# Keys and values of the second cross attention projected in the first one and kept in DRAM, and the first attention's tiles done two by two

## The reference

```python
def xattn0(x, ctx, mask):          # 4 heads of 64
    q = x @ Wq; k, v = split(ctx @ Wkv)
    s = where(mask, q k^T * 64**-0.5, -inf)
    return softmax(s) v @ Wo
def xattn1(x, ctx):                # 16 heads of 16, no mask
    q = x @ Wq1.T + bq; k = ctx @ Wk1.T + bk; v = ctx @ Wv1.T + bv
    return softmax(q k^T * 16**-0.5) v
x = x + xattn0(layernorm(x), ctx, mask)
x = x + gated_delta_net(layernorm(x))
x = x + top1_experts(layernorm(x))
x = x + xattn1(layernorm(x), ctx)
x = x + linear_attention(layernorm(x))
x = x + top2_experts(layernorm(x))
```

## Time and profile before

| | us |
|---|---|
| median of 3 runs | 1309.65 |
| lowest and highest | 1301.12, 1310.67 |
| profiled execution, its own time | 1307.67 |
| its span, first to last instruction | 1305.9 |
| first attention, first T to last value | 9 to 397 |
| delta net and first experts | 398 to 560 |
| second attention, preparation | 560 to 633.6 |
| its first load issued by SP, in the first experts | 543.9 |
| second attention, chunks 0 to 13 | 633.6 to 1251 |
| rest | 1251 to 1306 |

### The profile page before, as it was taken

The page is one execution under the profiler, slowest core; times in us unless marked ns, Lnnn a source line. Parts: engine busy times, 40 slices in busy tenths (PEclk is TensorE's granted clock), DMA queues, the critical chain, the costliest instruction groups (busy, mean ns, idle before and its releaser), DMA issues. The chain is left out here.

```text
span 1305.9 us, 25471 instructions
## 1 busy us (share of the span) xinstructions
PE 1134.1 (87%) x9184; PEld 714.7 (55%) x9184; DVE 574.0 (44%) x1415; ACT 601.2 (46%) x1233; POOL 224.9 (17%) x257
## 2 busy tenths in 40 slices
PE   7999999999998379775689889988988988988966
PEld 4666666666666179541355554554555545555543
DVE  3333333333336984345146436534534633634524
ACT  2544455444555412331355545544645544645631
POOL 1000000000004342203123213303312312321000
PEclk9999999999998789797789989988988988989976
DMA  4233111400000000229975585566557557537000
GB/s 156 81 127 115 32 33 34 127 32 32 0 0 1 1 1 2 65 63 166 218 123 101 108 137 96 112 111 113 101 101 125 96 93 130 100 65 120 2 1 5
DMA packets 64879, 101.98 MB, mean 78 GB/s; under 512 B 14366, under 2 KB 55350, under 8 KB 62102
## 3 DMA queue, kind: packets, MB, share of 16 engines
q1 hardware_dynamic: 64790, 100.67, 38.0%
HBM read 80.32 MB, written 19.60 MB: 77 GB/s over the span
## 5 line engine op out<-in xcount | busy, mean ns | idle before, releaser
L1539 DVE TENSOR_REDUCE mx<-bank 128x1 f32<-128x512 f32 (+1 forms) x448 | 257.2, 618 | 223.3 <-PE bank L1432 222.3
L1621 ACT ACTIVATE p<-bank 128x512 f32<-128x512 f32 x392 | 234.3, 598 | 180.6 <-PE bank L1470 174.7
L1470 PE MATMUL bank<-qrows,krows 99*128 99x128 bf16 x1568 | 161.2, 228 | 45.1 <-DMA qrows<-n3T 35.1
L1484 PE MATMUL bank<-p,v 128*32 128x128 f32 x3136 | 172.7, 293 | 19.6 <-issue 16.2
L1432 PE MATMUL bank<-krows,qrows 96*128 96x512 bf16 (+1 forms) x448 | 161.0, 363 | 13.7 <-DMA krows<-kscr 10.9
L1470 PEld LDWEIGHTS bank<-qrows,krows 99*128 99x128 bf16 x1568 | 116.3, 101 | 95.6 <-issue 52.4
L1303 POOL TENSOR_TENSOR kt<-kf,kt 128x512 bf16<-128x512 f32 (+1 forms) x52 | 53.7, 1034 | 449.6 <-ACT kt L1605 449.6
L1484 PEld LDWEIGHTS bank<-p,v 128*32 128x32 f32 x3136 | 63.4, 110 | 117.9 <-issue 88.6
L468 DVE CUSTOM_DVE_ANT_0 sc<-bank,pen 128x448 f32<-128x448 f32 x112 | 65.7, 620 | 113.9 <-issue 113.9
L1415 PE MATMUL bank<-ctxT,WT 128*128 128x512 f32 (+1 forms) x224 | 97.2, 557 | 3.7 <-ACT kt L1605 1.7
L1440 PE MATMUL bank<-WT,ctxT 128*128 128x256 f32 x392 | 98.2, 391 | 2.1 <-ACT v L1295 1.4
(11 more groups left out here) (292 smaller groups left out, 1449.7 us busy)
## 6 DMA issues: line engine op xcount, KB each, us to landing
ctx<-ctx SPq DMA_DIRECT2D x28, 896.0 KB, 10.8
krows<-kscr SPq DMA_DIRECT2D x84, 256.0 KB, 8.5
krows<-kscr SPq DMA_DIRECT2D x84, 192.0 KB, 6.9
kscr<-kt SPq DMA_DIRECT2D x14, 768.0 KB, 3.6
kscr<-kt SPq DMA_DIRECT2D x14, 576.0 KB, 13.0
ew<-L_ffn_expert_w SPq DMA_DIRECT2D x1, 2048.0 KB, 10.6
ew<-L_ffn_We SPq DMA_DIRECT2D x1, 2048.0 KB, 15.9
mask<-mask_BxSxS_bf SPq DMA_DIRECT2D x14, 112.0 KB, 5.2
```

The lines of the kernel that those rows point to most:

```text
L1470: ins = pe.matmul(bank[ST1[u % 2]][:, i * P:(i + 1) * P], krows[half][:, s, krow(h), cols], qrows[:, s, h, :], start=True, stop=True)
L1484: ins = pe.matmul(bank[OT1][32 * i:32 * i + 32, j * P:(j + 1) * P], v1[:, s, t, h * (D1 + 1):h * (D1 + 1) + 32], p1[:, u % 4, i * P:(i + 1 ...
L1539: dve.tensor_reduce(mx1[:, h, half:half + 1], bank[SM1[k % 3]][:, 0:HW[half]], AX.X, ALU.max).then_inc(S("smread1"), 1)
L1621: act.activation(p1[:, u % 4, :], bank[ST1[u % 2]][:], ACT.Exp).then_inc(S("exp1"), 1)
```

## The change

1. In the first attention, for each chunk, four operations J0 to J3 are added (keys of the second attention, 512 and 384 columns; ACT adds the bias and writes `kf`, POOL makes all three bf16 parts), and V becomes V0 to V6, one per tile and 512 columns wide (256 of the first attention's values, 256 of the second's), each copied out by two ACT copies. SP stores each chunk's key parts and values to DRAM, for all 14 chunks.
2. Per step, tiles go in pairs: the sides of two tiles, two `turn_exps`, two `values`. K, J and V share the two `KV` banks, 15 operations a chunk.
3. The second attention has no T, K, V, no context load and no store. `krows` and `v1` have three slots. `l1_loads`, in the first experts, gathers all of chunks 0, 1 and 2. S is one operation per head over both halves (two banks, one DVE reduction of 896 columns). Units go in pairs. The chunk loop is written out. M of the next chunk stands in pair 8 of 14; S8 to S15 of the next chunk in pairs 0 to 6, S0 to S7 of the one after it in pairs 7 to 13.
4. The weights of the second attention are loaded and turned at the start of the first.

```diff
+        PLAN0 = ((("T0", "T1"), ("T2", "T3")), (("K0", "K1"), ("K2", "K3")), (("S0", "S1"), ("J0", "S2", "S3")),
+                 (("S4", "S5", "V0"), ("J1", "S6", "S7", "M0")), (("V1", "E0", "E1", "E2", "E3"), ("V2", "V3")),
+                 (("J2",), ("V4", "V5")), (("V6", "F0"), ("J3",)))
+        TPAIRS = ((0, 1), (2, 3), (4, 5), (6,))
...
+                def kv_free(op, c):
+                    i = KVO.index(op)
+                    if some(NKV * c + i - 1):
+                        pe.wait_ge(S("kvread0"), NKV * c + i - 1)
...
+                    elif op[0] == "J":
...
+                        for i in range(DC):
+                            ins = pe.matmul(bank[kv_bank(op, s)][:, 0:HW[half]], WTk[:, i, b * P:(b + 1) * P],
+                                            ctxT0[:, i, HO[half]:HO[half] + HW[half]], start=(i == 0), stop=(i == DC - 1))
...
-                        for t in range(nt):
-                            for i in range(DC):
-                                ins = pe.matmul(bank[KV[k % 2]][:, t * D:(t + 1) * D],
-                                                ctxT0[:, i, (t0 + t) * P:(t0 + t + 1) * P], Wkv0[:, i, D:2 * D],
+                        for i in range(DC):
+                            ins = pe.matmul(bank[kv_bank(op, s)][:], ctxT0[:, i, k * P:(k + 1) * P],
+                                            Wv01[:, i].rearrange("p w o -> p (w o)"),
...
+                    for ts in TPAIRS:
+                        for t in ts:
+                            for op in PLAN0[t][0] + PLAN0[t][1] if ahead else ():
+                                side(op, c + 1, 1 - s, n + s)
+                        for t in ts:
+                            if t + 2 < CT:
+                                turn_exps(c, s, t + 2)
+                        for t in ts:
+                            values(c, s, t)
...
         def l1_loads(sp):
+            gather(sp, 0, 0)
+            gather(sp, 0, 1)
             for half in range(2):
                 sp.dma_start(krows[half][KROWS:KONES].rearrange("p s h (r c) -> p (s h r) c", c=P),
-                             onesb[KROWS:KONES].unsqueeze(1).to_broadcast([3, 2 * H1 * HT[half], P])
+                             onesb[KROWS:KONES].unsqueeze(1).to_broadcast([3, R1 * H1 * HT[half], P])
                              ).then_inc(S("krows_ones"), 16)
+            fetch_values(sp, 0)
+            for c in range(1, R1):
+                gather(sp, c, 0)
+                gather(sp, c, 1)
+                fetch_values(sp, c)
...
+                for c in range(NCH):
+                    if R1 <= c + 2 < NCH:
+                        sp.wait_ge(S("st1"), UNITS * c)
+                        gather(sp, c + 2, 1)
+                        sp.wait_ge(S("pv1"), UNITS * c)
+                        fetch_values(sp, c + 2)
+                    if c + 1 < NCH:
+                        rows(c + 1)
                     if c + 3 < NCH:
+                        sp.wait_ge(S("st1"), UNITS * c + HT[0] * 4)
+                        gather(sp, c + 3, 0)
...
+                def score(c, h):
+                    r, b = c % R1, sm_bank(("S", c, h))
+                    if h == 0:
+                        for half in range(2):
+                            pe.wait_ge(S(f"krows{half}_{r}"), 16 * NJ * (c // R1 + 1))
```

More of the change, by code:

```diff
@@ L507, in _ @@
                 penalty(0, 0, 0)
[L508 removed]
+                for op in PRO0:
                     side(op, 0, 0, 0)
@@ L560, in take_exps @@
                     act.wait_ge(S("pt0"), CT * c + t + 1)
-                    if some(CT * c + t - 1):
-                        act.wait_ge(S("pv0"), CT * c + t - 1)
-                    u = (s + t) % 2
-                    act.copy(pT0[:, u, :], bank[PT[u]][:]).then_inc(S("pT0"), 1)
-                for op in ALL0:
+                    was = CT * c + t - (2 if t < 3 else 3)
+                    if some(was):
+                        act.wait_ge(S("pv0"), was)
+                    act.copy(pT0[:, t % 4, :], bank[PT[(s + t) % 2]][:]).then_inc(S("pT0"), 1)
+                for op in PRO0:
                     side(op, 0, 0, 0)
@@ new lines, in sm_free @@
+                def sm_free(op):
+                    i = SMPOS[op] - 2
+                    if i >= 0:
+                        kind, c, h = SMSEQ[i]
+                        if kind == "S":
+                            pe.wait_ge(S("smread1"), H1 * c + h + 1)
+                        elif kind == "M":
+                            pe.wait_ge(S("n3T1"), c + 1)
+                        else:
+                            pe.wait_ge(S("acc1"), 2 * c + 3)
+                def score(c, h):
+                    r, b = c % R1, sm_bank(("S", c, h))
+                    if h == 0:
+                        for half in range(2):
+                            pe.wait_ge(S(f"krows{half}_{r}"), 16 * NJ * (c // R1 + 1))
+                    sm_free(("S", c, h))
+                    for half in range(2):
+                        ins = pe.matmul(bank[b + half][:, 0:HW[half]], qrows[0:KROWS, 0, h, :],
+                                        krows[half][0:KROWS, r, krow(h), :], start=True, stop=True)
+                    ins.then_inc(S("sm1"), 1)
@@ L1425, in side, with scores @@
+                def side(kind, c, h):
+                    if kind == "S":
+                        score(c, h)
+                    elif kind == "M":
+                        turn_maximum(c)
+                    else:
+                        turn(c)
+                def scores(c, u):
+                    t, j, g = u // 4, u % 4, UNITS * c + u
+                    if u == 0:
+                        if c == 0:
                             pe.wait_ge(S("krows_ones"), 32)
-                        if isinstance(c, int) and c == 1 and k == 0:
+                        if c == 1:
@@ L1510, in _ @@
-                steps1(pe, step)
+                ln_pe(pe, "ln2", 4)
+                pe.wait_ge(S("ln2_hT"), 1)
+                for b in range(DC):
+                    for i in range(DC):
+                        ins = pe.matmul(bank[5][:, b * P:(b + 1) * P], WTq[:, i, b * P:(b + 1) * P],
+                                        hT[:, i, :], start=(i == 0), stop=(i == DC - 1))
+                ins.then_inc(S("q1_psum"), 1)
+                pe.wait_ge(S("qrows_in"), 16 * NJ)
+                for op in PRO1:
+                    side(*op)
@@ new lines, in _ @@
+                scores(0, 0)
+                scores(0, 1)
+                for c in range(NCH):
+                    for p in range(PAIRS):
+                        if p + 1 < PAIRS:
+                            scores(c, 2 * p + 2)
+                            scores(c, 2 * p + 3)
+                        elif c + 1 < NCH:
+                            scores(c + 1, 0)
+                            scores(c + 1, 1)
+                        for op in plan1(c, p):
+                            side(*op)
+                        values(c, 2 * p)
+                        values(c, 2 * p + 1)
@@ L1579, in step @@
+                ln_dve(dve, "ln2")
+                query()
+                for op in PRO1:
+                    side(*op)
+                for c in range(NCH):
+                    if some(c):
                         read_out(c - 1)
-                        rescale(c - 1, 1 - s)
-                    sides(side, ALL1, c, s, n, two, one)
-                steps1(dve, step)
+                    for p in range(PAIRS):
+                        for op in plan1(c, p):
+                            side(*op)
```

663 lines of the change are left out of this document (284 added, 379 removed), and 6 rows, old and new, of the table PLAN1.

## The result

The changed kernel takes 1315.98 us, the kernel before 1307.08 (medians of seven runs each on the same chip); the ratio is 1.0076, with a 95% interval of 1.0048 to 1.0104. The forecast was 1293 us, most likely faster. The measured time lies inside its range of 1248 to 1325; direction and likeliest case were wrong. The profiled execution took 1318.36 us, its span is 1316.6.

What follows compares the result with a forecast made beforehand. The prediction took both attentions to be PE-bound before the change, and the second paced by its gather cycle after. 1307.67 + 182 + 29 - 226 = 1292.7, so 1293 us, range 1248 to 1325.

Steps and rivals of the forecast that it cites:

- First attention, +182: First attention: added J and wider V paid in full on PE, 13 us more a chunk; +182 us, bounds +150 and +210.
- The +1 us a chunk for moved stalls: First attention: new PE waits for DVE and ACT, set against about 1.0 us of stalls before; +1 us a chunk.
- The pairs save nothing by themselves: First attention: pairing tiles keeps every instruction, so no gain from it, though stalls move.
- Preparation, +29: Before the second attention: stored queries wait behind a full queue, scores start at 662 against 633.6; +29 us, bounds +5 and +40.
- Second attention, -226: Second attention: 391 us against 617.4, with cycles of 29.3 us a chunk; -226 us, bounds -270 and -190.
- each chunk PE waits some 3 us in pair 7: Second attention: PE no longer bounds the stage and stands some 3 us a chunk at S0 for key gathers.
- the cost of code: Rival: the first attention's longer loop no longer stays resident and PE stalls for instructions; about +35 us, 1326, chance 0.08.
- the loop of S0, M, `rows` and gathers: Second attention: next gathers issue only after S0, M and `rows`, and the next S0 waits for them; 29.3 us a cycle.
- Slow gathers: Rival: gathers stay as slow as beside stores, 14 and 9.8 us a chunk, cycle 31.6; 1321, no change, chance 0.10.
- PE pacing: Rival: gathers run ahead and PE paces the second attention at 25.5 us a chunk; 1253, chance 0.13.
- The clock case: Rival: PE's clock stays at its lower level for most of each second-attention chunk, 36 us a chunk; 1361, chance 0.09.

Runs made afterwards that it cites:

- e5_singles: The changed kernel with the first attention's tiles done one by one instead of two by two: 1305.3 us, ratio 0.9987 to the kernel before.
- e3_wide: The changed kernel with the six key copies interleaved, so each gather of 16 rows spreads over 96 partitions: 1213.37 us, ratio 0.9264.
- e2_three: The changed kernel, fetching only three of six key copies from the fourth chunk on, half the gathers' bytes: 1239.62 us, ratio 0.9445.
- e13_queue4: The changed kernel, narrow gathers issued two by two from the fourth chunk on, at most four in the queue: 1310.19 us, ratio 1.0032.
- e1_pieces4: The changed kernel with `krows` padded, so gathers move 4-KB and 3-KB pieces instead of 16-KB and 12-KB ones: 1327.72 us, ratio 1.013.
- e14_queue6: As e13_queue4, but gathers issued three by three, up to six in the queue: 1308.55 us, ratio 1.0006.
- e8_dump: e3_wide plus another 1.57 MB a chunk, from the fourth on, copied to device memory behind the gathers: 1209.39 us, ratio 0.9257.
- e9_dumpsb: As e8_dump, but the extra 1.57 MB a chunk go to an unused SBUF tile, written wide: 1210.54 us, ratio 0.924.
- e6_both: e3_wide with chunk 1 fetched behind the query's reads and chunk 2 behind the first maxima's rows: 1181.47 us, ratio 0.9038.

## Why the prediction was wrong, by its own steps

- **First attention, +182: +188.8** (the last turn of outputs, L515, at 585.19 against 396.34). The mechanism was right: 1.8 us for four records of 512 columns, ACT and POOL covered, no stall for code in the loop. The +1 us a chunk for moved stalls was right too: PE's waits for DVE and ACT in the loop grew by 14 us in thirteen chunks. The sentence "The pairs save nothing by themselves", which e5_singles tested, says less than the runs do: the pairs cost 0.9 us a chunk, 11 us in all, and that is nearly the whole of this +1, which one line undoes. What was mis-sized is small: 13.6 us in front of the loop for 12.5, 172.2 in it for 169 (the working had 13.5 a chunk and 13 was taken; 13.2 was measured), 3.1 behind it for 1, where PE now waits 2.37 for ACT.
- **Preparation, +29: +36.1.** First `scores` at 858.47, less 188.8, against 633.6. The wait behind a full queue was seen, but its gathers were put at 131 GB/s, from one window of 4 us, and 119 was measured: the first S, at 831.30 less 188.8, came 3.5 us later than 639. From there to `scores` are 27.2 us where 23 was taken. The reductions are 1 us of that (two S every 2.12 us, 1.06 each for 0.99); the rest is that eight S of the second chunk stand ahead of `scores` in PE's order, and PE works on them until 858.5 without a wait for the maxima's rows.
- **Second attention, -226: -211.4** (858.47 to 1264.5, 406 us against 617.4). This is where the prediction failed. PE's own work was less than I took: 24.0 us a chunk at full clock, as e3_wide shows. The step "each chunk PE waits some 3 us in pair 7" failed in the changed kernel: no such wait is there. In its place are 59.5 us of stops for instructions, 5.4 a chunk, and 3.4 to 7.2 us at the lower clock behind each. I had such a stop before me in the earlier trace rows, saw "<-issue", and put such stops at nothing in the new chunk without giving a reason; the cost of code was priced only as a rival, and only for the first attention's loop. e2_three, e3_wide and e13_queue4 show that it is the instruction transfer behind the gathers. Yet the loop of S0, M, `rows` and gathers is real and just hidden: e13_queue4 has it at 30.6 us, where I had 29.3. There the mis-sized term is the gather: 25.0 us from issue to S0, where 12.5 + 9.0 + 2.0 + 0.4 = 23.9 had been taken. The first bytes' 2.0 and the semaphore's 0.4 were not measured by themselves in any run.
- **Sum.** 6.8 + 7.1 + 14.6 too little, and 2.8 gained behind the second attention, which I had left as it was: 1292.7 + 25.7 = 1318.4, the profiled execution's time. All three terms erred to the same side; the two larger errors came of taking the better reading (gathers at the rate of their best window, no stall but the one named). A forecast of a gain of 1.3% made of terms of 182 and 226 us could not carry that.
- **Rivals.** Their times were added to 1291, not to the forecast's 1292.7, so each is some 2 us too low. Slow gathers (1321, no change) came nearest, with a cycle of 31.6 against 31.3, but that is luck in part: the gathers were as slow as it says, yet the wait at S0 that it goes by did not occur, and the stops made up the cycle. PE pacing (1253) was not the changed kernel but became true once gathers were wide. The clock case had the right sign: 0.89 in the stage; but the lower clock followed the stops, it did not cause them. The first attention's loop stayed resident: in 150 to 575 us two instruction transfers of 0.02 MB together move, and none on the queue (q8) that PE's stops hang on.

## What to carry to other kernels

When a wait is marked as issue in the middle of a group of equal operations, look at what the DMA queues hold at that time: the engine may be starved of instructions behind the kernel's own transfers. Here both the loop of the kernel before (16.2 us) and the written-out code (59.5) were. A transfer of few neighbouring rows is worth spreading over the partitions before anything is moved or prefetched around it; here that was two slices and 8.1%, more than the whole change. And when operations are only regrouped, count not the instructions, which stay the same, but the work that stands between an operation and the one whose result or bank it waits for.

## What had not been expected of the hardware

- Gathers of sixteen rows of 16 KB to 16 neighbouring partitions move at 119 GB/s, the same rows to partitions six apart at 229.
- While twelve narrow gathers stood in the queue, no instruction transfer ran for 16 us or more (none in 1004 to 1023 and in 1039.5 to 1055.5), whether the pieces were 16 or 4 KB (e1_pieces4: none in 1010 to 1027). With at most four gathers in the queue two ran in the middle of the burst (e13_queue4, 1035.5 to 1041). The Trainium skill ("DMA: Bandwidth & Descriptors", section on queues, rings and completion order) says that a DMA engine goes round between its queues packet by packet. By that an instruction transfer would wait for one packet; e13_queue4 and e14_queue6 show a wait that follows the number of gathers in the queue. That wide gathers followed by as much other traffic (e8_dump, e9_dumpsb) hold nothing back fits if that traffic entered the queue only after the instruction transfer was asked for; this was not tried by itself, and stays open.
- GpSimd filling three partitions made VectorE operations of 0.41 and 0.29 us last 7.02 and 6.52.
- SP stood 20.4 us issuing two transfers of together 1008 small pieces, with twelve narrow gathers ahead of them in the queue, and 8.3 us for the same two with wide gathers ahead (e6_both). So what holds SP is at least in part the queue in front. The block around it could not end before.
